# Maxima over the first chunk's keys by differences of its halves, and two chunks' units taking turns in the second attention layer

## What is computed

```python
x = x + 0.5 * _L0_ffn_ref(_layernorm(x), W_gate, W_qkv)      # attention
x = x + _L0_attn_ref(_layernorm(x), gamma, beta, W_in, ...)  # recurrence and skip
x = x + 0.5 * _L0_ffn_ref(_layernorm(x), W_gate, W_qkv)      # attention
# in _L0_ffn_ref
idx = argmax(softmax(x @ W_gate.T))          # one head of 16 for each token
k_shared, v_shared = keys and values of that head (values times the gate)
att = softmax(causal(q @ k_shared.T / sqrt(hd)))   # 16 heads, all with the same keys
y = att @ v_shared
```

## Time and profile before

| | us |
|---|---|
| median of 3 runs | 901.45 (896.96 to 907.77) |
| the profiled execution | 904.45 |
| its span, first to last instruction | 902.7 |
| mean granted TensorE clock, as a share of 2.4 GHz | 0.963 |

### The profile page before, as it was taken

The page is one execution under the profiler, slowest core; times in us unless marked ns, Lnnn a source line. Parts: engine busy times, 40 slices in busy tenths (PEclk is TensorE's granted clock), DMA queues, the critical chain, the costliest instruction groups (busy, mean ns, idle before and its releaser), DMA issues.

```text
span 902.7 us, 18417 instructions
## 1 busy us (share of the span) xinstructions
PE 844.9 (94%) x6300; PEld 282.7 (31%) x6300; DVE 778.2 (86%) x2252; ACT 691.8 (77%) x1142; POOL 298.0 (33%) x566
## 2 busy tenths in 40 slices
PE   8889779989999999999999899999999999999997
PEld 6433222333222233222432233333332323222221
DVE  5888998889998988979878998899989999999920
ACT  1127556566998989968878877888779998999996
POOL 4117314443111432325642445643431125110110
PEclk9889788989999999999999999999999999999999
DMA  6110000101000000010010001000010000000000
GB/s 185 49 42 20 1 1 1 60 1 60 2 2 1 1 2 1 2 59 2 1 59 2 2 1 42 20 1 25 1 60 2 2 26 2 24 1 2 1 2 23
DMA packets 20235, 17.97 MB, mean 20 GB/s; under 512 B 4128, under 2 KB 20144, under 8 KB 20144
## 3 DMA queue, kind: packets, MB, share of 16 engines
q1 hardware_dynamic: 19328, 16.00, 5.8%
q10 hardware_dynamic: 816, 0.80, 0.3%
HBM read 10.24 MB, written 6.29 MB: 18 GB/s over the span
## 4 chain that ended last, share of the span: by engine, by line
PE 50%; DVE 24%; ACT 10%; issue 10%; POOL 3%; DMA 1%; SPq 0%; POOLq 0%; DVEq 0%; ACTq 0%
PE ps L1752 16%; PE ps L1718 10%; DVE ps L1442 9%; PE ps L1740 9%; DVE mxp L1439 8%; ACT probs L1217 7%; PE ps L1636 3%; ACT relu L1205 2%; DVE mxp L1442 2%; PE ps L1641 2%; PE ps L1684 2%; PE ps L1651 1%; PE ps L1691 1%; POOL u L926 1%; DVE stats L1261 1%
## 5 line engine op out<-in xcount | busy, mean ns | idle before, releaser
L1217 ACT ACTIVATE probs<-ps 128x1024 f32<-128x1024 f32 (+5 forms) x843 | 556.2, 736 | 103.1 <-PE ps L1740 99.1
L1439 DVE TENSOR_REDUCE mxp<-ps 128x1 f32<-128x512 f32 x512 | 320.4, 682 | 20.7 <-PE ps L1718 16.6
L1752 PE MATMUL ps<-probs,v_l 128*32 128x512 f32 (+3 forms) x2560 | 304.6, 552 | 3.4 <-POOL probs L960 0.8
L1740 PE MATMUL ps<-q_t,k_tl 50*128 50x512 f16 (+3 forms) x1280 | 244.5, 357 | 21.0 <-DMA q_t<-m_row 9.2
L1718 PE MATMUL ps<-k_tl,q_t 48*128 48x512 f16 (+3 forms) x1152 | 249.4, 354 | 10.9 <-DVE mxp L1442 3.9
L1442 DVE CUSTOM_DVE_ANT_0 ps<-ps,mask 128x384 f32<-128x384 f32 (+3 forms) x512 | 233.6, 524 | 11.7 <-PE ps L1718 9.9
L960 POOL TENSOR_SCALAR_AFFINE_SELECT probs<-probs 128x256 f32<-128x256 f32 x256 | 103.2, 417 | 337.5 <-ACT probs L1217 336.1
L1718 PEld LDWEIGHTS ps<-k_tl,q_t 48*128 48x128 f16 x1152 | 73.9, 95 | 181.3 <-DVE mxp L1439 60.9
L1740 PEld LDWEIGHTS ps<-q_t,k_tl 50*128 50x128 f16 x1280 | 65.2, 94 | 188.2 <-ACT probs L1217 84.3
L1442 DVE CUSTOM_DVE_ANT_0 ps<-ps,relu 128x512 f32<-128x512 f32 x128 | 85.6, 716 | 8.2 <-PE ps L1718 7.3
L1442 DVE DVE_READ_ACCUMULATOR2_ANT mxp<- 128x1 f32 x640 | 89.2, 139 | 0.0
(11 more groups left out here) (181 smaller groups left out, 603.6 us busy)
## 6 DMA issues: line engine op xcount, KB each, us to landing
q_t<-q_scratch SPq DMA_DIRECT2D x96, 64.0 KB, 2.1
q_scratch<-q_part SPq DMA_DIRECT2D x16, 256.0 KB, 2.1
x_sb<-in_L_attn_x_dram SPq DMA_DIRECT2D x4, 512.0 KB, 8.2
out_dram<-x_sb SPq DMA_DIRECT2D x4, 512.0 KB, 3.0
q_t<-m_row SPq DMA_DIRECT2D x64, 4.0 KB
wqkv_n<-in_L_ffn_W_qkv_dram ACTq DMA_DIRECT2D x1, 768.0 KB, 6.9
w_in_sb<-in_L_attn_W_in_dram SPq DMA_DIRECT2D x1, 384.0 KB, 6.0
w_skip_sb<-in_L_attn_W_skip_dram SPq DMA_DIRECT2D x1, 256.0 KB, 5.5
```

Source lines behind the costliest of these rows:

```text
L1217: last = a_.activation(out if len(banks) == 1 else out[:, n:n + 1, :], bank[:, :, P * i:QW], ACT.Exp, scale=SCALE / LIFT ** 2)
L1439: last = v_.tensor_reduce(to, scores, axis=AX, op=ALU.max)
L1740: last = mm(ps[:, BANK[e][n], P * i:QW], k_cols(ROWS_XM, hh, l, kt, P), q_rows(ROWS_XM, c, g, hh, P * i, QW - P * i), start=True, stop=True)
L1752: last = mm(out_bank[VW * hh:VW * hh + VW, P * i:QW], v_l[:, l, kt, :], probs[:, s % NB, hh, P * i:QW], start=j == 0, stop=j == key_tiles( ...
```

## The change

Chunk 1's maxima over chunk 0's keys: before, 16 banks of kind "part" a unit, each 512 keys wide. Now each query tile (`HALF_TILES`) takes the 512 keys as two halves of 256: the difference of the halves is a bank of kind "diff" that holds two heads side by side, and the scores against the second half are a bank of kind "over" with two pieces of 256. The difference keys `kh_tl` are made from chunk 0's own keys in `prepare(l, 0)`, by one more "dpack" and "dkeys" in each layer. Chunks 2 and 3 keep their pairs.

The second layer takes chunk 1, then the units of chunks 2 and 0 in turn, then chunk 3. The largest weight is found by a maximum of absolute values, without squares and root. The first chunk of x is loaded in two parts by two queues, and the other chunks only when the weights have landed. The side work's places and some of the planner's constants are others.

```diff
-WARM_UP = 5
+WARM_UP = 4
-    + [(1, c, g) for c in (1, 2, 0, 3) for g in range(NG)]
+    + [(1, 1, g) for g in range(NG)] + [(1, c, g) for g in range(NG) for c in (2, 0)] + [(1, 3, g) for g in range(NG)]
+HALF_TILES = (0, 1, 2, 3)
...
     for i in range(TC):
+        if c == 1 and i in HALF_TILES:
+            ahead.append((len(banks), i, None))
+            pair("over", 1, lambda par: [(h0 + par, i, QW // 2, QW // 2, h0 // 2 * (QW // 2)) for h0 in (0, 2)])
+            continue
...
-        banks[at - 4:at - 4] = [("diff", 1, [(h0 + par, i, 0, QW, 0)]) for par in range(2)]
+        banks[at - 4:at - 4] = [
+            ("diff", 1, [(h0 + par, i, 0, QW, 0)] if h0 is not None
+             else [(h + par, i, 0, QW // 2, h // 2 * (QW // 2)) for h in (0, 2)]) for par in range(2)]
...
-            ("kpack", l, c), ("keys", l, c)] + ([("dpack", l), ("dkeys", l)] if c == 1 else [])
+            ("kpack", l, c), ("keys", l, c)] + ([("dpack", l, c), ("dkeys", l, c)] if c < 2 else [])
...
-SIDE_WORK = [(-10, 5, prepare(0, 1)), (5, 5, [("bias",)]), (16, 23, [("size",)] + SPLIT), (28, 38, prepare(0, 2)),
-             (38, 38, prepare(0, 3)), (80, 101, branch(0)), (109, 123, prepare(1, 0)), (124, 130, branch(1)),
-             (134, 134, prepare(1, 1)), (153, 166, branch(2)), (166, 177, prepare(1, 2)), (180, 199, branch(3)),
-             (202, 212, prepare(1, 3))]
+SIDE_WORK = [(-9, 8, prepare(0, 1)), (18, 20, [("bias",)]), (20, 20, [("size",)] + SPLIT), (25, 31, prepare(0, 2)),
+             (38, 38, prepare(0, 3)), (89, 102, branch(0)), (104, 108, prepare(1, 0)), (123, 127, branch(1)),
+             (138, 147, prepare(1, 1)), (154, 156, branch(2)), (159, 168, prepare(1, 2)), (170, 213, branch(3)),
+             (218, 223, prepare(1, 3))]
...
-    "size": (0, [("DVE", 6400)]), "halve": (0, [("POOL", 1700)]),
+    "size": (0, [("DVE", 3600)]), "halve": (0, [("POOL", 1700)]),
-FIRST_X, FIRST_W = 6500.0, 8900.0
+FIRST_X, FIRST_W = 5500.0, 7600.0
-SAME_MODE, MAXIMA_FIRST, LOOK = 400, 500, 400
-AHEAD, LOSS = 12, (("PE", 0.75), ("DVE", 1.0), ("ACT", 1.0))
+SAME_MODE, MAXIMA_FIRST, LOOK = 400, 500, 300
+AHEAD, LOSS = 12, (("PE", 1.5), ("DVE", 1.0), ("ACT", 0.75))
...
-            sp.dma_start(bands(0), x[0, 0:QW, :].rearrange("(t p) d -> p t d", p=P)).then_inc(s_xld[0], 16)
+            sp.dma_start(bands(0)[:, 0:2, :], x[0, 0:2 * P, :].rearrange("(t p) d -> p t d", p=P)).then_inc(s_xld[0], 16)
+            sp.wait_ge(s_wqkv, 32)
...
                 if e[2] == 0:
                     own(g_.tensor_copy(k_first[:, :, :], k_in[:, :, :]))
+                    g_.tensor_tensor(k_diff[:, 0:2, :], k_in[:, 0:2, :], k_in[:, 2:4, :], op=ALU.subtract)\
+                        .then_inc(s_kd, 1)
...
+            act.dma_start(bands(0)[:, 2:4, :], x[0, 2 * P:4 * P, :].rearrange("(t p) d -> p t d", p=P))\
+                .then_inc(s_xld[0], 16)
...
-                    last = v_.tensor_tensor(to if n < DC else to.rearrange("p (a w) -> p a w", a=a), of, of, op=ALU.mult)
+                    last = v_.tensor_reduce(z_all[:, n:n + 1], of, axis=AX if n < DC else mybir.AxisListType.XY, op=ALU.max,
+                                            apply_absolute_value=True)
...
-                    v_.tensor_copy(z_sq[:, :], bank[:, 0:2]).then_inc(s_rd, 1)
-                    dve.wait_ge(s_zroot, 1)
-                    own(v_.tensor_scalar(z_mul[:, :], z_root[:, :], W_SIZE, None, ALU.mult))
-                    own(v_.reciprocal(z_rec[:, :], z_mul[:, :]))
+                    own(v_.tensor_scalar(z_rec[:, :], bank[:, 0:2], 1.0 / W_SIZE, None, ALU.mult))
+                    v_.reciprocal(z_mul[:, :], z_rec[:, :]).then_inc(s_rd, 1)
+                    dve.wait_ge(s_rd, FREED[e])
```

62 lines of the change are left out of this document (26 added, 36 removed).

## The result

The changed kernel takes **895.2 us** (median of 20 runs, 891.04 to 897.69) against 902.5 for the kernel before in the same session: a ratio of **0.990**, with a 95% interval of 0.987 to 0.992. The forecast was 880.5 us, a gain of 2.3%; measured, the changed kernel takes 1.0% less. The profiled execution took 895.15 us, its span 893.4.

A forecast was written before the change was run, and what follows sets the result against it. DVE was taken to bound the kernel, in full in the first layer's chunk 1 and in part elsewhere. -27.9 - 4.0 + 12 - 2, about 1 taken back, gave -21: 880.5 us, range 873 to 888, with the rivals 866 to 896.

The forecast's parts named there:

- The maxima: Chunk 1, both layers: masked maxima of 256 columns every 0.385 us replace plain 512-column reductions; -27.9 us of DVE, bounds -20 and -28.
- the largest weight: DVE's search for the largest weight: five reductions and two tiny ones take 3.6 us instead of 6.73; -4.0 us with idle time.
- The first layer's chunk 1: From the row of unit (0, 0, 3) to that of (0, 1, 3): shrinks from 109 to about 90 us, clock above 0.86.
- The start: Loading x's first chunk in halves gives about 1 us, POOL's extra dpack gives back 1 to 1.5; taken as 0 together.
- -27.9 - 4.0 + 12 - 2 = -21.9 on the path: Whole kernel: maxima, largest weight, DVE's idle time at the layers' boundary and turns added up; -21 after about 1 us of hand-overs.
- DVE's idle time at the boundary: Between the layers: DVE idles 13.5 us in the preparation chain of the second layer's chunk 1, 12 more than before; bounds 5 and 20.
- PE's figure says least: Reading of busy times: PE's 844.9 us says least, because matmuls are pipelined and their ends modelled.
- The turns: Second layer's chunks 2 and 0 in turn: PE waits less for rows; -2 us, bounds 0 and -6.
- The gain stops at ACT: Rival, chance 0.17: ACT's 16.7 us a unit bounds chunk 1, the gain is 9.2 us; 892 us.
- The boundary costs nothing: Rival, chance 0.09: DVE's idle time at the layers' boundary is no one's wait; -33, 869 us.
- The late keys with a falling clock: Rival, chance 0.06: PE waits at the layers' boundary and its clock falls, up to 35 us longer; 918.5, or 915 against the median.
- my signs of being wrong: DVE waiting over 0.1 us per relu; ACT 90% busy in chunk 1; chunk 3's stages growing; PE's boundary clock below 0.9.

The follow-up runs named there:

- side_work_of_before: Changed kernel planned anew with the side work at its old places, so the second layer's chunk 1 is prepared earlier; 912.9 us, ratio 1.011 to the kernel before.
- halves_with_order_of_before: Changed kernel with unit order, side work places and planner constants of before, planned anew, without turns; 905.4 us, ratio 1.003 to the kernel before.
- no_dummies_in_the_middle: Changed kernel, order kept, with 43 of the 121 dummy matmuls on PE left out; 897.8 us, ratio 0.994 to the kernel before.
- no_halves: Changed kernel with chunk 1's maxima again plain reductions of 512 columns, planned anew; 935.3 us, ratio 1.033 to the kernel before.
- choose_of_1_1_on_dve: Changed kernel, order kept, with the four sums of prod for the second layer's chunk 1 on DVE, not POOL; 895.2 us, ratio 0.989 to the kernel before.
- dve_more_in_0_1: Changed kernel, order kept, with five more 512-column reductions on DVE in each unit of the first layer's chunk 1; 905.8 us, ratio 1.003 to the kernel before.
- pe_more_in_0_3: Changed kernel, order kept, with 60 more matmuls of 512 columns on PE in the first layer's chunk 3; 901.2 us, ratio 0.999 to the kernel before.
- dve_less_in_1_1: Changed kernel, order kept, DVE reading 64 of 256 columns in the halves' maxima of the second layer's chunk 1; 892.0 us, ratio 0.988 to the kernel before.
- act_less_in_1_1: Changed kernel, order kept, ACT making 128 of 512 columns of the relus in the second layer's chunk 1; 895.6 us, ratio 0.990 to the kernel before.

## Why the prediction was wrong

**The work was counted rightly.** The maxima (0.39 us apart, no wait for relus), the largest weight (3.52 us), ACT's +26 (I had 31 less 1 to 12), PE's +2.7 (0 to 2), and reductions from 512 to 384. The Trainium skill, "VectorE: DVE Perf Modes", section on the TRN2 errata, has 120 + FD cycles at 0.96 GHz from PSUM, an estimate of 0.39 us for 256 columns; the trace agrees for these maxima with their read, at 0.39, and not for the plain reductions of 512, 0.603 against its 0.66.

**The first layer's chunk 1 came out as forecast, in part by luck.** 109 to 91 us between the rows, and 17.8 us less up to its last exponential: 13.5 in the piece itself and 4.3 ahead of it. The start is not where these 4.3 come from: x's statistics begin at 4.87 us, 1.3 earlier, but the row of (0, 0, 3) comes at 77.5 us, and before at 77.1. The clock was 0.85 between the rows against 0.86, where I had expected a rise, and 0.91 against 0.86 between the last exponentials. I estimate that some 5 of the 13.5 us go with it: at 0.86 of 123.8 us the full clock is missed by 17.3 us, at 0.91 of 110.3 us by 9.9, and the changed kernel's runs at 0.969 and 0.977 lie 5.2 us apart for 7.1 us of the same. My sum had nothing for the clock.

**The step that failed is the sum**, "-27.9 - 4.0 + 12 - 2 = -21.9 on the path". It takes every microsecond of DVE at its full price and as kept to the end of the kernel. It rests on a reading of busy shares ("an edit that takes work from DVE pays in full in the first layer's chunk 1 and in part elsewhere"), of which even the second half was dropped in the sum. And it takes DVE's idle time at the boundary as lost time. The runs show otherwise. DVE relieved of 11 us in the second layer's chunk 1 is worth 4, not 11, so that the halves' 14 us there were worth an estimated 5. DVE's gap of 18 us at the boundary costs next to nothing: PE was busy 24.0 of 25 us in it, and a gap of 4 us in side_work_of_before did nothing for the exponentials.

These two errors have opposite signs, -14 + 12 forecast and -5 + 0 by the runs, and by themselves would have made the gain larger than forecast, not smaller. What made it smaller is the third: up to (0, 1, 3) forecast and result agree, at 18 us; for the rest I had 4 us of gain, and 8.6 of loss came, 4.7 of them more work of PE and 3.9 more idle time of PE. So the step that brought the miss is that a lead won in one stage was taken as kept to the end.

**What is left is that the lead was not kept.** Of 17.8 us at (0, 1, 3), 8.6 were gone at the end, and in halves_with_order_of_before 24.6 of 23.4. From there on PE, with scores, values, maxima and side work, idles 2 to 6% in both kernels, and the three engines are 80 to 95% busy over the run. That PE's stream and the hand-overs among the three hold the scores is my reading, and only in part shown: 9 us more on PE cost 8 to 10, the most of any engine, but 8.6 us less of dummies gave nothing, and 18 less on PE, together with DVE and ACT, gave 12 (9 to 11 at the same clock). My sentence "PE's figure says least" threw away the view that showed how little room PE had. So did leaving out one view altogether, the chain of waits by engine. Page, part 4, before:

```profile
PE 50%; DVE 24%; ACT 10%; issue 10%; POOL 3%; DMA 1%; SPq 0%; POOLq 0%; DVEq 0%; ACTq 0%
```

and after:

```profile
PE 55%; DVE 19%; issue 10%; ACT 8%; POOL 7%; DMA 0%; POOLq 0%; SPq 0%; DVEq 0%; ACTq 0%
```

DVE stands in that chain with 24% of 902.7, 217 of its 778 us: 0.28 of each. ACT stands in it with 10%, 0.13 of each of its 692. By this the 29 to 32 us taken from DVE would have been worth 8 to 9, and the 26 put on ACT would have cost 3: a third of my sum at most. By the chain after (0.19 x 893.4 / 749.1 = 0.23) the 22.5 us of the two kernels with less on DVE alone would be worth 5; they gave 3. This argument was made afterwards and is not a law. For work that was added the chain's share is too small (a microsecond cost 0.5 to 0.9 on DVE, and 0.6 on ACT in the first layer's chunk 1). And it fails where the change gained most: in the kernel before, from 96.9 to 220.7 us, DVE has some 26% of the chain for 111.7 us of work, again 0.28 of each (its four lines there are 11.0, 10.1, 2.8 and 1.7%), so that the 16.7 us by which its work fell in that piece would have been worth 5; 13.5 came, some 8 without what goes with the clock.

**The turns** were taken at -2 us with bounds of 0 and -6. With the halves, and with a new plan, they are worth 0.8%, about 7 us; without halves, planned anew too, nothing.

**The rivals.** "The gain stops at ACT" gave 892 us, nearest to the result, by a reason that holds in half at most: in the first layer's chunk 1, 10 us more on ACT now cost 6 at the same clock, nearly what they cost on DVE (7 to 8); but relieving ACT in the second layer gave nothing, and ACT is busy 68.47 of the 91 us between the rows. "The boundary costs nothing" was right on the boundary, and its 869 us wrong for the same cause as mine. The late keys with a falling clock didn't come: PE's clock in 452 to 563 is 0.98. Of my signs of being wrong one came in part, that the stages of chunk 3 grow: from 178.0 to 185.0 us in the first layer by the last exponentials and from 139 to 141 in the second by the rows, while by the other cut of each they fell. Where PE lost its dummies, in no_dummies_in_the_middle, the clock fell by 0.006 over the run and 1.4 us were lost where 9 were to be won. The Trainium skill, "TensorE: Matmul & The Clock Gate", section on HAM oscillation, has gaps in PE's work put the clock back; the run agrees in direction, at a price far below that rival's 35 us.

**Still open.** Which work ate the 8.6 us behind (0, 1, 3) was not traced to single waits. Why a list is granted more or less clock was not tested, though the kernels' median clocks range from 0.942 to 0.977 and over half of the measured gain goes with it. Why planning anew moves the time by 1 to 4% beside what was edited (no_halves, side_work_of_before) was not traced to a rule of the planner. ACT alone with less work in the first layer's chunk 1 was not run. No version here that computes all of the reference beats the changed kernel; choose_of_1_1_on_dve is level with it.

## What to carry to other kernels

Before counting a saving to the end of the kernel, ask for each later stage whether the lead will be kept there. Where three engines are over 80% busy, 9 to 11 us taken from one alone were worth 0 to 4, while 7 to 10 added cost 6 to 10. The engine's share in the chain that ends last was nearer to this than its busy share, but it was found afterwards, and it is too low where DVE was the one tight engine. Follow the work whose end is the kernel's end (here the exponentials), not the engine that was relieved: DVE was 25 us ahead at the boundary and the scores 16. Test a part with the order kept; a scheduler's new plan can move more than the part does. And compare runs with the same granted clock, or a few microseconds of clock are taken for the work's.

## What the runs showed of the hardware that was not expected

The time of one program follows the clock that is granted to it in a run; in the kernels with 12 runs or more it is 4 to 9 us for 0.01. The changed kernel took 891.0 us at a mean granted clock of 0.977, 894.5 at 0.972 and 897.7 at 0.969; dve_more_in_0_1 took 898.8 at 0.976 and 906.8 at 0.962. In all the kernels the clock is at its lower level for part of the first 150 us, also where PE idles little. The table by stage of the changed kernel, 90 to 120 us, with the clock at 0.64 and PE busy 27.34 of 30:

```profile
90.00:120.00 30.00, 27.34 (x184) 10.95 (x180) 24.01 (x101) 17.93 (x31) 8.83 (x17) 0.64 0.01 2
```

PE's busy time is elastic. 60 matmuls of 512 columns more, 12.8 us at 2.4 GHz, made PE's busy time 6.9 us longer in pe_more_in_0_3: half of them went into time that the page already called busy.

With the order kept, two runs of different kernels agree to 0.1 to 0.7 us at every row until the edit begins where the clock falls alike: dve_less_in_1_1 and the changed kernel have the row of (0, 3, 3) at 452.0 and 452.1 us. Where the clock falls otherwise, 90 to 120 us having 0.50 in act_less_in_1_1 and 0.64 in the changed kernel, the last exponential of (0, 1, 3) comes at 205.2 us instead of 202.9 with no edit before it. So one profile can tell 1 us from 0 only where the clocks of the stretch are alike.
